# Local attention blocks: a full-width stream transpose and four ScalarE copies in place of four stream transposes

## The reference, cut to what matters

```python
for i in range(DEPTH):                                  # DEPTH = 6
    x = attn_layer(shift_tokens(x), Wqkv[i], ...) + x
    x = ffn_layer(shift_tokens(x), ...) + x

def local_attention(q, k, v):                           # 16 heads of 64, windows of w = 32 tokens
    bk2, bv2 = look(bk), look(bv)                       # the window before, and the own one: 64 keys
    sim = einsum('bhwie,bhwje->bhwij', bq, bk2) * QK_SCALE
    attn = softmax(where(mask, -max, sim), -1)
    return einsum('bhwij,bhwje->bhwie', attn, bv2)
```

## Time and profile before

| | us |
|---|---|
| median of 3 runs | 3904.56 (3898.9 to 3905.77) |
| span of the profiled execution | 3896.6 |
| VectorE busy | 3022.0 (78%) |
| ScalarE busy | 2012.2 (52%) |
| TensorE busy | 3299.6 (85%) |
| GpSimd busy | 1097.2 (28%) |

### The profile page before, as it was taken

The page is one execution under the profiler, slowest core; times in us unless marked ns, Lnnn a source line. Parts: engine busy times, 40 slices in busy tenths (PEclk is TensorE's granted clock), DMA queues, the critical chain, the costliest instruction groups (busy, mean ns, idle before and its releaser), DMA issues. The chain is left out here.

```text
span 3896.6 us, 71287 instructions
## 1 busy us (share of the span) xinstructions
PE 3299.6 (85%) x25164; PEld 1850.2 (47%) x25164; DVE 3022.0 (78%) x3833; ACT 2012.2 (52%) x2780; POOL 1097.2 (28%) x610
## 2 busy tenths in 40 slices
PE   5999999999965788878787878887878787878997
PEld 2222222222234555555555555555555555547886
DVE  3777777777734989898989898989898988955664
ACT  1455555555532656665666565656556565631111
POOL 2000000000012545354535453544353444410000
PEclk6999999999976999999999999999999999988998
DMA  3000000000021100110010001000100110010000
GB/s 108 12 15 16 14 14 15 15 15 14 15 92 38 41 22 28 30 42 23 28 45 27 22 27 45 27 21 23 50 27 17 33 28 22 22 33 1 0 0 28
DMA packets 70709, 107.04 MB, mean 27 GB/s; under 512 B 26790, under 2 KB 41012, under 8 KB 69684
## 3 DMA queue, kind: packets, MB, share of 16 engines
q1 hardware_dynamic: 69716, 104.37, 9.3%
q10 hardware_dynamic: 864, 0.79, 0.1%
HBM read 38.79 MB, written 15.73 MB: 14 GB/s over the span
## 5 line engine op out<-in xcount | busy, mean ns | idle before, releaser
L918 DVE TENSOR_REDUCE a_part_max<-a_ps_max 128x1 f32<-128x512 f32 x1024 | 683.1, 690 | 290.5 <-PE a_ps_max L840 288.6
L816 ACT ACTIVATE a_expT<-a_ps_scoresT 128x1024 f32<-128x1024 f32 x512 | 516.8, 1024 | 315.6 <-PE a_ps_scoresT L852 310.0
L861 PE MATMUL a_ps_out<-a_expT,a_v_op 128*32 128x512 f32 x2048 | 537.6, 605 | 0.6 <-issue 0.5
L1204 POOL TENSOR_TENSOR b_turned_q<-b_rot_q,b_turned_q 128x1024 f32<-128x1024 f32 x96 | 226.8, 2363 | 925.8 <-DVE b_turned_q L1540 925.8
L1618 DVE STREAM_TRANSPOSE b_probsT<-b_probs 32x1024 f32<-32x1024 f32 x384 | 474.6, 1236 | 14.1 <-POOL b_probs L1220 2.0
L840 PE MATMUL a_ps_max<-a_k_op,a_q_op 96*128 96x512 bf16 x1024 | 401.5, 392 | 25.0 <-DMA a_k_op<-terms_k 21.1
L840 PEld LDWEIGHTS a_ps_max<-a_k_op,a_q_op 96*128 96x128 bf16 x1024 | 98.3, 96 | 515.5 <-DVE a_part_max L918 428.5
L1420 PE MATMUL b_psD<-b_probsT,b_v 128*64 128x128 f32 x3072 | 337.9, 278 | 5.8 <-DVE b_probsT L1618 5.8
L1421 PE MATMUL b_psD<-b_probsT,b_v_back 128*64 128x128 f32 x3072 | 332.9, 274 | 0.0
L1435 PE MATMUL b_psD<-b_w_qkv,b_xs 128*128 (+1 forms) x384 | 215.1, 648 | 116.7 <-ACT b_outT L1284 116.7
L1370 PE MATMUL b_psQ<-b_w_qkv,b_xs 128*128 (+1 forms) x384 | 194.2, 629 | 138.6 <-DVE b_xs L1498 138.6
(11 more groups left out here) (292 smaller groups left out, 6259.2 us busy)
## 6 DMA issues: line engine op xcount, KB each, us to landing
b_v_back<-b_v SPq DMA_DIRECT2D x96, 384.0 KB, 3.5
b_v_back<-b_v SPq DMA_DIRECT2D x96, 128.0 KB, 3.4
b_w_qkv<-L_ffn_Wqkv SPq DMA_DIRECT2D x6, 1536.0 KB
sums<-a_outT SPq DMA_DIRECT2D x512, 16.0 KB
j_got<-sums SPq DMA_DIRECT2D x16, 512.0 KB
a_q_op<-terms_q SPq DMA_DIRECT2D x64, 48.0 KB
a_k_op<-terms_k SPq DMA_DIRECT2D x64, 48.0 KB
b_w_o<-L_ffn_Wo SPq DMA_DIRECT2D x6, 512.0 KB
```

The lines of the kernel that those rows point to most:

```text
L816: act.activation(expT[kt % RING][:], ps_scoresT[kt % 2][:], ACT.Exp, scale=SCALE_A).then_inc(exp_ready, 1)
L861: last_mm = pe.matmul(ps_out[lo:lo + 32, :], v_op[(u // 2) % 2][:, kt, :], expT[kt % RING][:, 512 * half:512 * half + 512], start=(kt < 2) ...
L918: dve.tensor_reduce(part_max[:, qt, half:half + 1], ps_max[half][:], AX.X, ALU.max).then_inc(max_taken, 1)
L1204: pool.tensor_tensor(turned[:], rot[:], turned[:], ALU.add).then_inc(added, 1)
```

## The change

VectorE does a single stream transpose over all 128 partitions, into a new tile `packed` with the layout of `probs` (each 32x32 block turned in its place). ScalarE copies the four 32-partition slices of `packed` to the diagonal blocks of `probsT`. It does so in the next step, between its qT copies and `square_q`; it waits for `packed_ready` and for `out_half` of the tile before. VectorE's transpose now waits for the copies of the previous `packed` (`probsT_ready`), and its subtraction into `probs` for `packed_ready` instead of `probsT_ready`. The layer-norm scaling of the `ahead` step, which stood behind the first of the four transposes, stands behind the one.

```diff
--- before.py
+++ after.py
@@ -984,6 +984,7 @@
         row_max = sb("row_max", [P, HEADS_B])
         row_sum = sb("row_sum", [P, HEADS_B])
         inv_sum = sb("inv_sum", [P, HEADS_B])
+        packed = sb("packed", [P, HEADS_B, 2, W])
         probsT = sb("probsT", [P, 2, HEADS_B, P])
         outT = sb("outT", [P, PAIRS, P])
 
@@ -1043,6 +1044,7 @@
         sum_ready = sem("sum_ready")
         inv_sum_ready = sem("inv_sum_ready")
         probs_ready = sem("probs_ready")
+        packed_ready = sem("packed_ready")
         probsT_ready = sem("probsT_ready")
         out_half = sem("out_half")
         outT_held = sem("outT_held")
@@ -1257,6 +1259,13 @@
                     for half in range(2):
                         act.wait_ge(qT_half, 2 * (T - 1) + half + 1)
                         act.activation(qT[:, 4 * half:4 * half + 4, :].rearrange("p a b -> p (a b)"), psD[half][:], ACT.Copy).then_inc(qT_held, 1)
+                if 2 in lags:
+
+                    act.wait_ge(packed_ready, T - 1)
+                    act.wait_ge(out_half, 2 * (T - 2))
+                    for j in range(P // W):
+                        rows = slice(W * j, W * j + W)
+                        act.activation(probsT[rows, :, :, rows].rearrange("p c h q -> p h c q"), packed[rows], ACT.Copy).then_inc(probsT_ready, 1)
                 if 0 in lags:
 
                     act.wait_ge(q_ready, T + 1)
@@ -1570,7 +1579,7 @@
 
                     dve.wait_ge(max_ready, T)
                     if 2 in lags:
-                        dve.wait_ge(probsT_ready, 4 * (T - 1))
+                        dve.wait_ge(packed_ready, T - 1)
                     rows = probs[:].rearrange("p h c k -> p h (c k)")
                     dve.tensor_tensor(rows, scores, row_max[:].unsqueeze(2).to_broadcast([P, HEADS_B, 2 * W]), ALU.subtract).then_inc(shifted_ready, 1)
                 if 0 in lags:
@@ -1612,12 +1621,10 @@
 
                     dve.wait_ge(probs_ready, T)
                     if 2 in lags:
-                        dve.wait_ge(out_half, 2 * (T - 1))
-                    for j in range(P // W):
-                        rows = slice(W * j, W * j + W)
-                        dve.transpose(probsT[rows, :, :, rows].rearrange("p c h q -> p h c q"), probs[rows]).then_inc(probsT_ready, 1)
-                        if j == 0 and ahead:
-                            scale(ahead[0], ahead[1], 0)
+                        dve.wait_ge(probsT_ready, 4 * (T - 1))
+                    dve.transpose(packed[:], probs[:]).then_inc(packed_ready, 1)
+                    if ahead:
+                        scale(ahead[0], ahead[1], 0)
                 elif ahead:
                     scale(ahead[0], ahead[1], 0)
                 if 2 in lags and not ahead:
```

## The result

The changed kernel takes 4040.09 us (4039.21 to 4041.85, four runs) beside 3903.55 us (3898.9 to 3905.77, four runs) of the kernel before: 1.0352 times as long, with a 95% interval of 1.0337 to 1.0367, or 136.5 us more. The forecast was 4041 us, slower.

A forecast was written before the change was run, and what follows sets the result against it. VectorE was taken as the bound, its relief turned into a loop through ScalarE: 72 plain steps at +1.48, 11 at +0.58, 11 at +2.13 and 0.5 give +137 us; span 4033, time 4041 us, range 3992 to 4095.

The forecast's parts named there:

- The transpose: VectorE, each step: one full-width transpose at 1.24 us replaces four taking 5.04, so 3.80 us less.
- Rival 5: VectorE: the full-width transpose does the quarters in turn, 5.04 us; +3.80 more a step, about 4400 us; chance 0.03.
- The copies: ScalarE, each step: four added copies of 1.06 us, 1.083 apart without overlap, 4.31 us; bounds 3.9 and 4.9.
- Rival 3: ScalarE's four copies: narrow ones are cheap, so not slower; break-even 0.71 us each, at 0.5 near 3840 us; chance 0.05.
- rival 1: ScalarE's four copies overlap like full-width ones, 3.95 us; 34 us less, 4007 us; chance 0.15.
- The loop: Plain step, VectorE to ScalarE and back: transpose, copies, `square_q`, to its reduction; 6.65 us for 5.28, +1.37.
- What is late next: Plain step behind `square_q`: kT copies start later, `square_k` reaches VectorE 0.11 us late; scores covered with about 1.1 to spare.
- the sum: Whole kernel: 72 plain steps at +1.48, 11 at +0.58, 11 at +2.13, last tile +0.5; +137 us.
- The other two kinds of step: Tile before an MLP +0.58 us, first tile after one +2.13, 11 each; transposes removed before the MLP give nothing back.
- Rival 2: TensorE's clock falls as it waits ahead of the scores: +0.3 to +0.5 us a step, 4070 to 4085 us; chance 0.10.
- The prediction's sign of being wrong: Changed profile: the forecast is wrong if, among other signs, the clock of plain steps is no longer 1.00.
- Rival 4: VectorE's relief counts in full, 94 x 3.80 = 357 us, about 3548 us; needs copies out of `square_q`'s way; chance 0.02.

The follow-up runs named there:

- same_slice: Changed kernel with all four ScalarE copies reading and writing partitions 0 to 31 only, so slices 1 to 3 are left out of the result: 3986.51 us.
- wide_copies: Changed kernel with each of the four ScalarE copies taking all 128 partitions of `packed`, filling `probsT` outside its diagonal too: 3991.18 us.
- two_copies: Changed kernel with only two of the four ScalarE copies made, the other two diagonal blocks of `probsT` staying 0: 3839.82 us.
- the GpSimd runs: Changed kernel with all four copies on GpSimd, 3802.31 us, or also with xs copies early, 3811.07; copies shared with ScalarE, xs early: 3712.34, 3695.19, 3673.87.
- copies_pool: Changed kernel with all four copies made by GpSimd behind its `rot_k` products instead of by ScalarE: 3802.31 us, 0.9734 of the kernel before.

## Why the prediction was right, step by step

**The transpose** was taken at 1.24 us with bounds of 1.21 and 5.04; the 96 of them average 1245 ns. Rival 5 is out.

**The copies** were taken at 1.06 us, 1.083 apart, 4.31 in all; they average 1054 ns and take 4.29. Rival 3 (cheap narrow copies) and rival 1 (overlap) are out. The reason given was only half right: "work on a slice of the partitions" loses the overlap. `same_slice` has slices and overlaps, at 3.90 us; it is the change of first partition that costs it, here 0.12 to 0.13 us at each of four borders (three between copies, one to `square_q`). kT in the earlier trace rows alternates halves, so its four copies, 24 ns between each end and the next start, were the right row to go by. The Trainium skill (ScalarE: Activation LUTs, What ACT_TABLE_LOAD costs) gives an overlap of about 93 ns between back-to-back ACTIVATEs, beside figures measured on tiles of 128 partitions, and names no such condition. An estimate by it is 1.06 + 3 x 0.964 = 3.95 us. `wide_copies` and `same_slice` come near it with 3.90, the changed kernel's 4.29 does not.

**The loop** was forecast at 6.65 us and took 6.73. The only term that missed by more than 0.02 is the hand-over from VectorE to ScalarE, 0.11 for 0.03: it had been read off a hand-over inside ScalarE, which knows nothing of the other engine's signal.

**What is late next.** `square_k` was to come 0.11 late. It does not: `square_q` and the first kT copy overlap (2111.32 against an end of 2111.42), which the sum had with a gap of 0.02, so `square_k` ends 3.37 us after `square_q`'s end (2114.79 less 2111.42), not 3.50, and VectorE waits for it 1.1 us in all 96 tiles together. The two misses, +0.08 and -0.11, nearly cancel: plain steps are 21.19 us for 21.20.

**The other two kinds of step.** The steps into the tile before an MLP are 21.11 to 21.19 us for 20.61 to 20.64 before: +0.52 for +0.58. First tile after an MLP: from `centred` to the reduction of `square_k` 25.32 us (2047.09 to 2072.41) for 23.42 before (1998.36 to 2021.78): +1.90 for +2.13. Two overlaps of 0.1 make the difference, of the first copy with the qT copies (2063.66 against an end of 2063.77) and of kT with `square_q`. And the transposes taken out ahead of the MLP gave nothing back, as argued: the wait of 2.42 became 6.71.

**What the sum lacked.** One wait, found in the groups by form. Before:

```profile
L1513 DVE TENSOR_TENSOR b_centred<-b_zs,b_psS 128x512 f32<-128x512 f32 x12 | 8.3, 688 | 10.5 <-PE b_psS L1330 10.1 <-issue 0.5
```

and after:

```profile
L1522 DVE TENSOR_TENSOR b_centred<-b_zs,b_psS 128x512 f32<-128x512 f32 x12 | 8.3, 688 | 23.0 <-PE b_psS L1339 19.6 <-issue 3.5
```

In the tile before an MLP VectorE also reads a product that TensorE makes behind the scores and the products with `probsT`, and these now come later: 12.5 us more in 12 readings. Of that, 4.1 are in the last tile (a wait of 6.08 before, 10.16 after), where the wait only takes the place of the transposes that are gone. The other 8.4 are in the eleven MLPs between tiles, 0.77 each. In the MLP of the earlier trace rows the reading begins 9.69 us after the reduction of `square_q` for 9.06 before, and the scaling that opens the MLP follows 10.3 us behind it in both kernels. The sum followed TensorE to the row maximum and stopped there.

So the hit to 1 us is partly luck. The spans of the two profiled executions differ by 141.6 us, not 137, and of that 1.5 lies ahead of the first tile, where nothing was changed. The forecast took the run's time as its span plus 8.0 us. The profiled execution of the kernel before was its fastest, 2.3 over its span (3898.9), and that of the changed kernel lies 2.1 over its own (4040.27 against 4038.2).

**Rival 2** (the clock) came true as a mechanism and hardly as a cost. TensorE's mean granted clock went from 0.950 to 0.932, with waits of 2.81 us ahead of the scores (foreseen were 3.2 less the 0.6 of the band product), and in 49 of the 82 steps above part of the scores run at the lower level. From the first to the last score is then about 3.2 us in most steps, for 2.31 at 1.00. But the row maximum starts at 2094.73 without a wait in the step with the 1.66 us above: the 1.1 us of room that the prediction counted for the scores covered it. The room ran out in four tiles, whose maximum waited 0.16 to 0.19 us behind scores of up to 3.6 us; the longest of the 82 steps is 21.36. In all 96 tiles the row maximum waits 10 us for TensorE, but 8.91 of these are in the last tile (4.68 before), again in place of the transposes. The prediction's sign of being wrong, a clock of plain steps no longer at 1.00, did appear and cost next to nothing. **Rival 4** (relief in full) is what `two_copies` and the GpSimd runs approach from afar, and what the order forbids.

Open: why GpSimd needs the time that it does around each copy (four copies of 1.03 us take 5.3) was not taken apart.

## What to carry to other kernels

Work moved off the busiest engine helps only if it isn't queued between that engine and its next input: follow the order of the receiving engine from the moved work to the next thing that the relieved engine reads, and add up that loop. Where the receiving engine's slack lies ahead of an instruction that waits for something else, the slack is no use to work that becomes ready only behind it. Look for short copies whose duration depends on their neighbour: moving two of them up by three operations gave more here (161 us) than the packed transpose, shared copies and the move of `square_k` did together on top of it (67 us more).

## What the hardware showed that was not expected

**ScalarE's overlap depends on the first partition.** Copies of 1.04 to 1.06 us start 0.95 to 0.96 us apart where the next begins at the same partition as the one ahead (32, 64 or 128 partitions), and 1.06 to 1.08 apart where it begins at another. The number of partitions decides neither the overlap nor, within 0.02 us, the duration. Whether the partition read or the one written counts is open: in all these runs the two are the same. The same holds against neighbours of another kind: `square_q` behind the last slice (partition 96) starts 0.02 after it, behind a copy from partition 0 it starts 0.1 before its end.

**A VectorE copy is held until GpSimd's running instruction ends.** The xs copies took 0.21 us with GpSimd idle and 1.04 and 2.28 beside it; GpSimd's timeline in the kernel before:

```profile
2087.57 1.90 POOL L1220 TENSOR_TENSOR b_probs<-b_probs,b_inv_sum 128x1024 f32<-128x1024 f32 x1 [1.75 <-DVE b_inv_sum L1588]
2089.43 2.35 POOL L1204 TENSOR_TENSOR b_turned_k<-b_rot_k,b_turned_k 128x1024 f32<-128x1024 f32 x1
```

The first xs copy ends at 2089.54, the division at 2089.47; the second at 2091.86, the addition at 2091.78. The reductions and the transposes beside the same kind of work keep their 1.21 and 1.25 us. The Trainium skill (SBUF — State Buffer, Who interferes with whom) says that copies and `tensor_scalar` in a two-port mode share a port pair with GpSimd, held for a whole instruction, and that on this chip `tensor_reduce` never contends. The traces agree on both, with `floored` (a `tensor_scalar`, 0.17 us in `copies_pool`, 1.31 above) too; which mode the copies ran in they don't show.
